# Groups of x centred by GpSimd, their maximum and rounding on VectorE a slot later, in a gated cross-attention and feed-forward block

## The chip, the core and the metric

The kernel runs on one core of a Trainium2 chip. The metric is device microseconds from the start to the end of one execution. The five engines have their own queues of instructions and run in order, each on its own: PE (TensorE), DVE (VectorE), ACT (ScalarE), POOL (GpSimd) and SP (SyncE, which here only issues transfers). They wait for each other by semaphores alone.

## What is computed

The reference, cut to what matters:

```python
x = x + tanh(g_xattn[0]) * xattn(layernorm(x), ctx, ctx)   # 32 batches, 112 rows, 256 wide; 375 keys; 16 heads
x = x + tanh(g_ffn[0]) * ffn(layernorm(x))

def ffn(x):                               # bitlinear: x -> 1024 (gate and up) -> 256
    return bitlinear(silu(bitlinear(x, w_gate)) * bitlinear(x, w_up), w_down)
def bitlinear(x, w):
    return einsum(act_quant(x), weight_quant(w))
def act_quant(x):                         # per row, to 255 levels
    scale = 127 / max(|x|)
    return clip(round(x * scale), -128, 127) / scale
```

The rows of the second layer normalisation are 32 x 112 = 3584, that is 28 tiles of 128 rows. A row is centred (its mean is taken off), and the levels are the rounded quotients of the centred row and a 127th of its largest magnitude. The standard deviation only enters the scale, later.

## The kernel before, in words

**Time is a table of slots.** All engines run through the same function `timeline`: slot t = 8n + p, where row n is a batch and p one of its eight slots (two heads each), from t = -16 to 302 and on; each engine issues in slot t what the code of that slot gives it, in the order in which it is written. The attention has two passes. The first (scores, their maximum, exponentials and statistics; L1328, L926, L1197, L907) ends with slot 257. The second (transposed scores L1369, exponentials L1187 into `pt`, weighted values L1348) runs 26 slots behind it, up to slot 282. Behind both come the batch's last steps, each in a fixed slot p: `ot` is copied (p = 2, L916), the output projection (p = 3, PE L1415), the new rows x2 are written (p = 4, DVE L885), the heads are turned back (p = 5, PE L1433), normalised (p = 6, DVE L891 and L895, the tile `on`), and POOL makes `onn`, `on` and `ong` (p = 7, L684, L685, L689: "the trio"). The value projections stand in p = 6, 7 and 0 on PE (L1407) and are copied a slot later by DVE (L859, the tile `va`); all of these use one PSUM bank `p_m`, in turn.

**The groups.** While the second pass runs out (slots 258 to 285, from 641 us on), the 28 row tiles of x2 are read back in groups of two tiles and made into levels. Groups 0 to 11 (`EARLY_GROUPS` + 1 = `TAILED` = 12 of them) are spread over the slots, group i from slot X_AT + 2i = 258 + 2i, by `group_at(t, lag)`; what follows for a group is at a fixed lag:

- lag -3: SP loads it into `xl` (part of the tile `ctxt`), two buffers (`load_group`, L457)
- lag 0: DVE takes the mean off (L990, into `fxn`, part of the tile `ex`), takes the largest magnitude of each row (L996, `xmax`), makes the scale (L998, `xsc`) and its inverse (L1000, `xinv`) (`x_group`)
- lag 1: ACT multiplies by the inverse and adds a large number, which rounds (L1233, `round_group`, in place)
- lag 2: POOL takes that number off again and writes bf16 (L728, `quant_group`, into `fxq`, part of `qp`)
- lag 3: PE transposes four blocks (L1485, `transpose_group`)
- lag 4: DVE copies them out of PSUM (L1015, `copy_group`, into parts of `kp`, `kf` and `ctxt`)

**The feed-forward** runs by tiles: `tile(0)` to `tile(7)` stand between slots 284 and 308 (`BETWEEN`), the others follow. In `tile(s)`: PE multiplies tile s by the gate and up weights (L1492), ACT makes silu (L1250, `sg`), DVE the product (L1032, part of the tile `kst`) and its row maximum (L1035), after every second tile also the scale and inverse (L1040, L1042); ACT rounds tile s - 2 (L1257), POOL takes the number off (L744), SP transposes by a DMA, and six tiles later PE multiplies by the third weights (L1524), ACT scales (L1243), POOL adds the residual (L751). For the last seven tiles DVE does that (L1053).

**The two late groups**, 12 and 13 (tiles 24 to 27), stand in the feed-forward: `LATE_AT = {10: 12, 13: 13}` puts the same steps of `x_group` at tile 10 and 13 of DVE, the rounding one tile later, and so on. For these DVE takes the mean off by another instruction, a scalar-tensor-tensor that adds a column of zeros in PSUM (L992), with a memset of that column before the first.

## Time and profile before

| | |
|---|---|
| median of three runs | 793.21 us (792.26 to 796.49) |
| the profiled execution | 792.8 us, its span 791.0 us |
| mean granted clock of TensorE, share of full speed | 0.962 |
| DVE busy | 708.0 us (90% of the span) |
| PE busy | 702.7 us (89%) |
| ACT busy | 683.9 us (86%) |
| POOL busy | 487.9 us (62%) |

The profile is of one execution. "Busy" is the time in which an instruction of the engine runs; the busy shares are means over stages with different limits. In the stage of the groups (640 to 688 us) all engines have gaps; in the feed-forward (688 to 781 us) DVE has nearly none. The page's map of the span in 40 slices of 19.8 us shows this (each digit the busy tenths): the last nine digits of DVE are 776798995, those of POOL 043245663.

### The profile page before, as it was taken

How to read it: one execution, taken by the hardware profiler on the slowest of the kernel's cores; microseconds unless marked ns; L12 is line 12 of the kernel's file. 1: busy time of each engine (PE TensorE's matmuls, PEld its weight loads, DVE VectorE, ACT ScalarE, POOL GpSimd, SP SyncE). 2: the span in 40 equal slices, each digit the busy share in tenths (PEclk: the TensorE clock that was granted, in tenths of full speed). 3: DMA queues.
4: the chain of work that ended last, by engine and by line, in shares of the span. 5: the costliest groups of instructions: out<-in, count | busy, mean ns of one | idle time of the engine just before them, and what ended most of it. 6: DMA issues, size and time to landing. Idle time of an engine off the chain costs nothing.

```text
span 791.0 us, 20866 instructions
## 1 busy us (share of the span) xinstructions
PE 702.7 (89%) x7118; PEld 474.6 (60%) x7127; DVE 708.0 (90%) x1452; ACT 683.9 (86%) x1454; POOL 487.9 (62%) x956
## 2 busy tenths in 40 slices
PE   6567899999999999999999999999999888877896
PEld 4334566666666666667676766676765555533453
DVE  5779899989899999999999999899999776798995
ACT  1578899898999999999999999999999888768883
POOL 4747657667777667676766666767664043245663
PEclk9666899999999999999999999999999899999998
DMA  9997747464668575767455666656664122246688
GB/s 206 204 261 166 197 127 149 109 126 128 154 120 149 124 144 124 145 122 158 123 138 134 134 137 133 128 136 130 124 118 85 39 68 86 71 103 164 160 179 181
DMA packets 148887, 108.50 MB, mean 137 GB/s; under 512 B 56991, under 2 KB 145183, under 8 KB 148767
## 3 DMA queue, kind: packets, MB, share of 16 engines
q1 hardware_dynamic: 143630, 101.98, 58.3%
q10 hardware_dynamic: 5152, 5.19, 2.7%
q8 instruction: 57, 0.93, 0.6%
q14 instruction: 48, 0.39, 0.2%
HBM read 49.54 MB, written 12.85 MB: 79 GB/s over the span
## 4 chain that ended last, share of the span: by engine, by line
PE 36%; ACT 35%; DVE 16%; issue 9%; DMA 2%; ACTq 1%; POOL 1%; SPq 0%; DVEq 0%; POOLq 0%
ACT ex L1197 13%; ACT pt L1187 12%; PE p_o L1348 7%; PE p_m L1426 6%; PE p_s L1328 5%; PE p_m L1407 5%; PE p_t L1369 4%; DVE kst L1032 3%; DVE hmax L1035 3%; PE p_m L1415 3%; ACT L1223 3%; ACT L1187 2%; DVE stats L907 2%; PE p_m L1399 2%; DVE nm L926 2%
## 5 line engine op out<-in xcount | busy, mean ns | idle before, releaser
L1197 ACT ACTIVATE ex<-p_s,nm 112x375 f32<-112x375 f32 x512 | 275.8, 618 | 12.3 <-DVE nm L926 11.0
L1187 ACT ACTIVATE pt<-p_t,ct 128x336 f32<-128x336 f32 x488 | 245.8, 577 | 26.7 <-PE p_t L1369 24.5
L907 DVE BATCH_NORM_STATS2 stats<-ex 112x6 f32<-112x375 f32 x512 | 252.5, 535 | 1.4 <-ACT ex L1197 1.3
L926 DVE TENSOR_REDUCE nm<-p_s 112x2 f32<-112x750 f32 x256 | 236.0, 922 | 1.2 <-PE p_s L1328 1.0
L1328 PE MATMUL p_s<-kst,qst 96*112 96x375 bf16 x512 | 154.8, 348 | 13.5 <-ACT ex L1197 7.3
L1369 PE MATMUL p_t<-qst,kst 99*128 99x112 bf16 x1464 | 115.1, 213 | 4.9 <-ACT pt L1187 4.0
L1369 PEld LDWEIGHTS p_t<-qst,kst 99*128 99x128 bf16 x1464 | 91.1, 98 | 44.0 <-issue 19.7
L1407 PE MATMUL p_m<-wv_sb,ctxt 128*128 128x256 f32 (+1 forms) x384 | 106.7, 401 | 4.7 <-DVE va L859 2.9
L1348 PE MATMUL p_o<-pt,va 128*32 128x112 f32 (+1 forms) x3072 | 101.7, 265 | 1.4 <-ACT pt L1187 0.8
L1426 PE MATMUL p_m<-ctxt,wk_sb 128*128 128x375 f32 x240 | 94.6, 518 | 1.7 <-DVE qf L875 1.1
L1328 PEld LDWEIGHTS p_s<-kst,qst 96*112 96x112 bf16 x512 | 67.0, 139 | 45.7 <-ACT ex L1197 34.6
L1348 PEld LDWEIGHTS p_o<-pt,va 128*32 128x32 f32 (+1 forms) x3072 | 70.4, 110 | 29.3 <-issue 27.0
L1407 PEld LDWEIGHTS p_m<-wv_sb,ctxt 128*128 128x128 f32 (+1 forms) x384 | 66.7, 190 | 20.4 <-DVE va L859 10.3
L859 DVE TENSOR_TENSOR va<-p_m,bv_sb 128x256 f32<-128x256 f32 (+1 forms) x96 | 40.0, 417 | 27.4 <-PE p_m L1407 26.6
L1426 PEld LDWEIGHTS p_m<-ctxt,wk_sb 128*128 128x128 f32 x240 | 44.3, 199 | 28.2 <-DVE x L885 7.5
L572 POOL TENSOR_SCALAR kp<-kf 128x375 bf16<-128x375 f32 x63 | 32.8, 521 | 43.9 <-ACT kf L1130 43.9
L578 POOL TENSOR_TENSOR kp<-kf,kp 128x375 bf16<-128x375 f32 x63 | 55.3, 878 | 5.2
L574 POOL TENSOR_TENSOR kf<-kf,kp 128x375 f32<-128x375 f32 x63 | 55.1, 875 | 5.3
L1492 PE MATMUL p_s<-wq,kp 128*128 128x512 bf16 x161 | 41.1, 380 | 12.6 <-DVE kst L1032 10.0
L744 POOL TENSOR_SCALAR kst<-kst 128x1024 bf16<-128x1024 f32 (+1 forms) x28 | 28.9, 1032 | 28.4 <-ACT kst L1257 28.3
L1257 ACT ACTIVATE kst<-kst,hinv 128x1024 f32<-128x1024 f32 (+1 forms) x29 | 32.1, 1115 | 9.0 <-DVE hinv L1042 9.0
L1032 DVE SCALAR_TENSOR_TENSOR kst<-p_s,usc,kst 128x1024 f32<-128x1024 f32 x28 | 35.9, 1282 | 3.6 <-ACT kst L1250 3.3
(187 smaller groups left out, 1164.3 us busy)
## 6 DMA issues: line engine op xcount, KB each, us to landing
kst<-kp SPq DMA_DIRECT2D x378, 93.8 KB, 3.5
ctxt<-ctxt_dram SPq DMA_DIRECT2D x32, 375.0 KB, 4.2
qbounce<-qp SPq DMA_DIRECT2D x32, 168.0 KB, 2.5
qst<-qbounce SPq DMA_DIRECT2D x32, 168.0 KB, 3.6
qst<-qbounce SPq DMA_DIRECT2D x32, 112.0 KB, 3.4
xm<-x_dram SPq DMA_DIRECT2D x32, 112.0 KB, 2.4
x_dram<-x SPq DMA_DIRECT2D x32, 112.0 KB, 1.9
xt<-x_dram SPq DMA_DIRECT2D x28, 128.0 KB, 3.2
```

The source lines that it names most:

```text
L574: nc.gpsimd.tensor_tensor(kf[:, c], kf[:, c], hi, ALU.subtract).then_inc(s_kx, 1)
L578: nc.gpsimd.tensor_tensor(lo, kf[:, c], mid, ALU.subtract).then_inc(s_kp2, 1)
L907: last = nc.vector.bn_stats(stats[:, nb % RING, 2 * pb + i], ex[0:SQ, 2 * (t % 2) + i, :])
L926: nc.vector.tensor_reduce(nm[:, n % RING, 2 * p:2 * p + 2], p_s[t % 2][0:SQ, :, 0:SK], axis=AX.X, op=ALU.max, negate=True).then_inc(s_max, 1)
L1032: nc.vector.scalar_tensor_tensor(out=hh[n % HHRING].rearrange("p (b k) -> p b k", b=2), in0=p_u[:, :, :], scalar=usc[:, n:n + 1], in1=sg[n ...
L1187: nc.scalar.activation(pt[:, (2 * r + i) % 8], st_home(r, i)[:, 0:KC * SQ].rearrange("k (c q) -> k c q", c=KC), ACT.Exp, scale=ct[:, nr % ...
L1197: nc.scalar.activation(ex[0:SQ, 2 * ((t - 1) % 2) + i, :], p_s[(t - 1) % 2][0:SQ, i, 0:SK], ACT.Exp, bias=nm[:, ne % RING, h:h + 1]).then_ ...
L1328: scores = mm(p_s[t % 2][0:SQ, i, 0:SK], qst[n % KRING][0:STACK, h, :], kst[n % KRING][0:STACK, h, 0:SK], start=True, stop=True)
L1348: last = mm(o_acc[VW * i:VW * (i + 1), grp, :], va[ng % VRING][0:KEYS[c], c, 4 * grp + i, :], pt[0:KEYS[c], (2 * (g - 1) + i) % 8, c, :], ...
L1369: last = mm(st_home(r, i)[:, c * SQ:(c + 1) * SQ], kst[nr % KRING][:, h, c * KR:(c + 1) * KR], qst[nr % KRING][:, h, :], start=True, stop= ...
L1407: last = mm(p_m[0:KEYS[ch], 0:D], ctxt[:, v % CRING, k, ch * KR:ch * KR + KEYS[ch]], wv[:, k, :], start=(k == 0), stop=(k == C - 1))
L1426: last = mm(p_m[:, 0:SK], wk[:, k, c * P:(c + 1) * P], ctxt[:, f % CRING, k, :], start=(k == 0), stop=(k == C - 1))
```

## The change

- POOL gets a new `centre_group` at lag 0: the two negated means of the group (128x2, L728 of the changed kernel; they are written into the columns of `xinv` that the inverses take later), then two tensor-scalars of 128x256, "add the negated mean, times 1.0", from `xl` to `fxn` (L737 there). It stands behind `quant_group` of the group before in the same slot.
- DVE's `x_group` moves from lag 0 to lag 1 and no longer takes the mean off. For groups 0 to 11 it then rounds the group itself, with two tensor-scalars of 128x256 in place, in the same slot. ACT's `round_group` is gone for them.
- The late groups: POOL centres them at tile 10 and 13, DVE takes maximum, scale and inverse at 11 and 14, ACT rounds at 12 and 15, POOL quantises at 13 and 16, PE transposes at 15 and 18, DVE copies at 16 and 19. The column of zeros and its memset are gone.
- SP's wait before loading group i is for the centring of group i - 2, as it was, but now POOL's.

```diff
@@ POOL, slot(t)
                 i = group_at(t, 2)
                 if i is not None:
                     quant_group(i)
+                i = group_at(t, 0)
+                if i is not None:
+                    centre_group(i)
+
+            def centre_group(i):
+
+                of = slice(GROUP * i, GROUP * (i + 1))
+                pool.wait_ge(s_ag, GROUP * (i + 1))
+                nc.gpsimd.tensor_scalar(xneg[:, of], mv2[:, of, 0], -1.0, 0.0, ALU.mult, ALU.add).then_inc(s_neg, 1)
+                pool.wait_ge(s_gl[i % 2], ring_count(16 * GROUP, i, 2))
+                if i == 0:
+                    pool.wait_ge(s_bn, SLOTS * B)
+                if i >= 2:
+                    pool.wait_ge(s_gq, count(1, i - 2, 1))
+                pool.wait_ge(s_neg, count(1, i, 1))
+                for g in range(GROUP):
+                    k = GROUP * i + g
+                    last = nc.gpsimd.tensor_scalar(fxn[:, i % 2, g], xl[:, i % 2, g], xneg[:, k:k + 1], 1.0, ALU.add, ALU.mult)
+                last.then_inc(s_cen, 1)
@@ POOL, tile(s)
-                if s - 2 in LATE_AT:
-                    quant_group(LATE_AT[s - 2])
+                if s - 3 in LATE_AT:
+                    quant_group(LATE_AT[s - 3])
+                if s in LATE_AT:
+                    centre_group(LATE_AT[s])
@@ DVE, slot(t)
-                i = group_at(t, 0)
+                i = group_at(t, 1)
                 if i is not None:
                     x_group(i)
@@ DVE, x_group(i)
-                for g in range(GROUP):
-                    k = GROUP * i + g
-                    if i < TAILED:
-                        last = nc.vector.tensor_scalar(fxn[:, i % 2, g], xl[:, i % 2, g], mv2[:, k, 0:1], None, ALU.subtract)
-                    else:
-                        last = nc.vector.scalar_tensor_tensor(out=fxn[:, i % 2, g], in0=xl[:, i % 2, g], scalar=mv2[:, k, 0:1],
-                                                              in1=zero.to_broadcast([P, D]), op0=ALU.subtract, op1=ALU.add)
-                last.then_inc(s_gx, 1)
-                dve.wait_ge(s_gx, count(4, i, 1))
+                dve.wait_ge(s_cen, count(1, i, 1))
                 nc.vector.tensor_reduce(xmax[:, of], fxn[:, i % 2], axis=AX.X, op=ALU.max, apply_absolute_value=True).then_inc(s_gx, 1)
...
+                if i < TAILED:
+                    dve.wait_ge(s_gx, count(3, i, 3))
+                    for g in range(GROUP):
+                        k = GROUP * i + g
+                        last = nc.vector.tensor_scalar(fxn[:, i % 2, g], fxn[:, i % 2, g], xinv[:, k:k + 1], ROUND, ALU.mult, ALU.add)
+                    last.then_inc(s_gr, 1)
@@ DVE, tile(s)
-                if s in LATE_AT:
-                    x_group(LATE_AT[s])
+                if s - 1 in LATE_AT:
+                    x_group(LATE_AT[s - 1])
@@ ACT, slot(t)
-                i = group_at(t, 1)
-                if i is not None:
-                    round_group(i)
@@ SP, load_group(i)
-                    sp.wait_ge(s_gx, count(4, i - 2, 1))
+                    sp.wait_ge(s_cen, count(1, i - 2, 1))
```

How the instructions stand now, at the places of which the prediction speaks. DVE, slots 260 to 262, before (from the new rows of slot 260 to the normalised heads of slot 262; group 0 stands ahead of them):

```order
L885 SCALAR_TENSOR_TENSOR x<-p_m,tg_sb,xm 112x256
L901 RECIPROCAL fa<-fa 112x32
L990 TENSOR_SCALAR ex<-ctxt,mv 128x256 x2
L996 TENSOR_REDUCE xmax<-ex 128x2
L998 TENSOR_SCALAR xsc<-xmax 128x2
L1000 RECIPROCAL xinv<-xsc 128x2
L931 BN_STATS st<-xt 128x6
L936 BN_AGGR mv<-st 128x2
L891 RECIPROCAL rl<-p_m 112x16
L895 TENSOR_TENSOR on<-p_m,rl 112x256
```

The same stretch of the changed kernel:

```order
L906 SCALAR_TENSOR_TENSOR x<-p_m,tg_sb,xm 112x256
L922 RECIPROCAL fa<-fa 112x32
L952 BN_STATS st<-xt 128x6
L957 BN_AGGR mv<-st 128x2
L999 TENSOR_REDUCE xmax<-ex 128x2
L1001 TENSOR_SCALAR xsc<-xmax 128x2
L1003 RECIPROCAL xinv<-xsc 128x2
L1008 TENSOR_SCALAR ex<-ex,xinv 128x256 x2
L912 RECIPROCAL rl<-p_m 112x16
L916 TENSOR_TENSOR on<-p_m,rl 112x256
```

Group 1 has moved from slot 260 to slot 261, behind the statistics (`st`, `mv`) and still ahead of `rl` and `on` of slot 262; its first instruction now reads what POOL has centred, and it ends with the rounding.

POOL before, from the last feature (`fc`, slot 258) to the trio of slot 263 (`fd` is of slot 260, the first `qp` is group 0):

```order
L663 TENSOR_TENSOR fc<-fc,fe 112x32
L667 TENSOR_TENSOR fd<-fa 112x32
L670 TENSOR_TENSOR fd<-fd,fc 112x32
L728 TENSOR_SCALAR qp<-ex 128x512 x2
L684 TENSOR_SCALAR onn<-on 112x256
L685 TENSOR_SCALAR on<-on 112x256
L689 TENSOR_TENSOR ong<-onn,on 112x256
L728 TENSOR_SCALAR qp<-ex 128x512
```

POOL from the same place on, in the changed kernel:

```order
L663 TENSOR_TENSOR fc<-fc,fe 112x32
L728 TENSOR_SCALAR xinv<-mv 128x2
L737 TENSOR_SCALAR ex<-ctxt,xinv 128x256 x2
L667 TENSOR_TENSOR fd<-fa 112x32
L670 TENSOR_TENSOR fd<-fd,fc 112x32
L747 TENSOR_SCALAR qp<-ex 128x512
L728 TENSOR_SCALAR xinv<-mv 128x2
L737 TENSOR_SCALAR ex<-ctxt,xinv 128x256 x2
L747 TENSOR_SCALAR qp<-ex 128x512
L728 TENSOR_SCALAR xinv<-mv 128x2
L737 TENSOR_SCALAR ex<-ctxt,xinv 128x256 x2
```

The centring of group 0 stands between `fc` and `fd`, and each further centring behind the quantising (L747) of the group before it: the two alternate, through all twelve groups.

## Rows read from the trace of the kernel before

**Rows 1.** Busy time in four stretches of the groups' stage (busy us, count, by engine)

```profile
core 0: us, PE busy (x) PEld busy (x) DVE busy (x) ACT busy (x) POOL busy (x), PEclk, DMA share, GB/s
...
sum 48.00, PE 38.38 PEld 28.05 DVE 34.98 ACT 40.97 POOL 17.99; mean PE 9.60 PEld 7.01 DVE 8.74 ACT 10.24 POOL 4.50
```

**Rows 2.** Busy time in the feed-forward stage, same columns

```profile
688.00:781.00 93.00, 75.84 (x433) 40.83 (x440) 86.36 (x124) 72.98 (x86) 50.69 (x70) 1.00 0.66 152
```

**Rows 3.** Groups by form, ACT, 640 to 688 us (busy us, mean ns; idle before)

```profile
L1233 ACT ACTIVATE ex<-ex,xinv 128x256 f32<-128x256 f32 x24 | 10.9, 506 | 3.7 <-DVE xinv L1000 3.6
```

**Rows 4.** The chain that ended last, 640 to 690 us, by line

```profile
by line: ACT pt L1187 13.4%; issue 10.2%; PE p_o L1348 9.3%; DVE xmax L996 7.0%; DVE ex L990 6.4%; PE p_m L1415 6.3%; ACT ex L1233 4.8%; PE p_m L1407 4.1%; PE p_s L1369 3.7%; DVE kp L1015 3.2%; PE p_t L1369 3.1%; PE p_s L1485 2.8%; DVE kst 
```

**Rows 5.** Groups by form, DVE, 640 to 688 us

```profile
L996 DVE TENSOR_REDUCE xmax<-ex 128x2 f32<-128x512 f32 x12 | 8.2, 686 | 0.4
...
L990 DVE TENSOR_SCALAR ex<-ctxt,mv 128x256 f32<-128x256 f32 x24 | 7.7, 361 | 0.0
...
L998 DVE TENSOR_SCALAR xsc<-xmax 128x2 f32<-128x2 f32 x12 | 2.8, 237 | 0.4
...
L1000 DVE RECIPROCAL xinv<-xsc 128x2 f32<-128x2 f32 x12 | 2.0, 166 | 0.4
```

**Rows 6.** Groups by form, POOL, whole span

```profile
L678 POOL TENSOR_SCALAR xn<-xa,mv,rstd 112x256 f32<-112x256 f32 x28 | 34.3, 1226 | 0.0
...
L621 POOL TENSOR_SCALAR ltc<-lt 128x32 f32<-128x32 f32 x16 | 5.2, 324 | 14.7 <-ACT lt L1155 14.7
...
L654 POOL TENSOR_SCALAR fe<-fb 112x32 f32<-112x32 f32 x16 | 3.5, 218 | 1.4
...
L693 POOL TENSOR_SCALAR bo_sb<-bo_sb,tg_sb 128x256 f32<-128x256 f32 x1 | 0.5, 477 | 0.0
```

**Rows 7.** Timeline, all engines, 640 to 664 us (start us, us, engine, line)

```profile
641.36 0.61 DVE L990 TENSOR_SCALAR ex<-ctxt,mv 128x256 f32<-128x256 f32 x2
...
642.03 0.25 POOL L663 TENSOR_TENSOR fc<-fc,fe 112x32 f32<-112x32 f32 x1
...
644.15 0.48 DVE L885 SCALAR_TENSOR_TENSOR x<-p_m,tg_sb,xm 112x256 f32<-112x256 f32 x1 [1.05 <-PE p_m L1415]
...
644.55 0.34 DVE L901 RECIPROCAL fa<-fa 112x32 f32<-112x32 f32 x1
...
645.63 0.62 POOL L728 TENSOR_SCALAR qp<-ex 128x512 bf16<-128x512 f32 x1
...
647.33 0.42 DVE L895 TENSOR_TENSOR on<-p_m,rl 112x256 f32<-112x256 f32 x1
...
653.39 0.97 ACT L1187 ACTIVATE pt<-p_t,ct 128x336 f32<-128x336 f32 x2
...
657.86 0.39 DVE L916 COPY ot<-p_s 128x224 f32<-128x224 f32 x1 [1.73 <-PE p_s L1319]
```

**Rows 8.** Timeline, all engines, 664 to 692 us

```profile
664.85 1.13 PE L1407 MATMUL p_m<-wv_sb,ctxt 128*128 128x256 f32 x4 [0.34 <-DVE on L895]
...
682.57 0.73 POOL L631 TENSOR_TENSOR xm<-xm,bo_sb 112x256 f32<-112x256 f32 x1
...
682.62 0.70 DVE L998 TENSOR_SCALAR xsc<-xmax 128x2 f32<-128x2 f32 x1
...
684.67 0.39 DVE L916 COPY ot<-p_s 128x224 f32<-128x224 f32 x1 [0.77 <-PE p_s L1319]
...
687.31 1.45 PEld L1492 LDWEIGHTS p_s<-wq,kp 128*128 128x128 bf16 x8
```

**Rows 9.** Groups of lines, DVE, 640 to 688 us: copies of the values

```profile
L859 DVE TENSOR_TENSOR va<-p_m,bv_sb 128x256 f32<-128x256 f32 (+1 forms) x6 | 2.5, 418 | 3.6 <-PE p_m L1407 3.6
```

**Rows 10.** Groups of lines, DVE, 688 to 781 us

```profile
L992 DVE SCALAR_TENSOR_TENSOR ex<-ctxt,mv,p_t 128x256 f32<-128x256 f32 x4 | 1.7, 477 | 0.0
...
L998 DVE TENSOR_SCALAR xsc<-xmax 128x2 f32<-128x2 f32 x2 | 1.1, 532 | 0.1
```

**Rows 11.** Transfers, 640 to 690 us (KB, us from issue to landing)

```profile
ctxt<-x_dram SPq DMA_DIRECT2D x20, 128.0 KB, 2.2
```

More of the change, by code:

```diff
@@ L144, in gated_block @@
         xmax, xsc, xinv = sb("xmax", [P, TILES]), sb("xsc", [P, TILES]), sb("xinv", [P, TILES])
+        xneg = xinv
         gsc, usc = sb("gsc", [P, TILES]), sb("usc", [P, TILES])
@@ L214, in gated_block @@
         tail_ride = p_s[0][:, 1, 0:C * SQ].rearrange("p (c q) -> p c q", c=C)
-        zero = p_t[0][:, 511:512]
         p_g, p_u = p_s[0], p_s[1]
@@ L263, in gated_block @@
         s_sc0, s_raw, s_raw2, s_smallw = sem("s_f_scaled_by_pool"), sem("s_f_unclipped"), sem("s_f_unclipped_by_pool"), sem("s_setup_weights")
-        s_zero = sem("s_zero_column")
+        s_neg, s_cen = sem("s_f_means_negated"), sem("s_f_x_centred")
         s_bn2, s_ln2, s_sq2 = sem("s_f_bn"), sem("s_f_ln"), sem("s_f_sqrt")
@@ L967, in rows_scale @@
                 dve.wait_ge(s_ln2, count(3, j, 2))
-                dve.wait_ge(s_gx, count(4, end // GROUP))
+                dve.wait_ge(s_gx, count(3, end // GROUP))
                 nc.vector.tensor_tensor(rstd2[:, first:end], rstd2[:, first:end], xsc[:, first:end], ALU.mult).then_inc(s_ln2, 1)
@@ L976, in x_group @@
                 of = slice(GROUP * i, GROUP * (i + 1))
[L977 to L995 removed]
+                dve.wait_ge(s_cen, count(1, i, 1))
                 nc.vector.tensor_reduce(xmax[:, of], fxn[:, i % 2], axis=AX.X, op=ALU.max, apply_absolute_value=True).then_inc(s_gx, 1)
[L997 removed]
+                dve.wait_ge(s_gx, count(3, i, 1))
                 nc.vector.tensor_scalar(xsc[:, of], xmax[:, of], XSC_MIN, 1.0 / 127.0, ALU.max, ALU.mult).then_inc(s_gx, 1)
[L999 removed]
+                dve.wait_ge(s_gx, count(3, i, 2))
                 nc.vector.reciprocal(xinv[:, of], xsc[:, of]).then_inc(s_gx, 1)
+                if i < TAILED:
[4 more added lines that the diff above has]
+                    last.then_inc(s_gr, 1)
             def copy_group(i):
@@ L1022, in tile @@
                     rows_scale(EARLY_TILES, TILES, 1)
-                if s - 5 in LATE_AT:
-                    copy_group(LATE_AT[s - 5])
+                if s - 6 in LATE_AT:
+                    copy_group(LATE_AT[s - 6])
                 n = s
@@ L1223, in slot @@
                     nc.scalar.activation(hid1[:, :], t_h1, ACT.Gelu, bias=b1[:, 0:1]).then_inc(s_g1, 1)
-                i = group_at(t, 1)
-                if i is not None:
-                    round_group(i)
             def round_group(i):
-                act.wait_ge(s_gx, count(4, i, 4))
+                act.wait_ge(s_gx, count(3, i, 3))
                 for g in range(GROUP):
@@ L1257, in tile @@
                         nc.scalar.activation(hr[n % HRING][:, half], hh[n % HHRING][:, half], ACT.Copy, scale=hinv[:, n:n + 1], bias=ROUND).then_inc(s_hr, 1)
-                if s - 1 in LATE_AT:
-                    round_group(LATE_AT[s - 1])
+                if s - 2 in LATE_AT:
+                    round_group(LATE_AT[s - 2])
                 if s == SQ_AT:
@@ L1530, in tile @@
                         nc.tensor.matmul(p_u[:, 0, :], identb[:, :], wq8[0][:, 0:512], start=True, stop=True)
-                if s - 4 in LATE_AT:
-                    if LATE_AT[s - 4] == TAILED:
+                if s - 5 in LATE_AT:
+                    if LATE_AT[s - 5] == TAILED:
                         pe.wait_ge(s_otc, B)
-                    transpose_group(LATE_AT[s - 4])
+                    transpose_group(LATE_AT[s - 5])
             timeline(slot, tile)
```

12 lines of the change are left out of this document (removed).

## The prediction

> **What bounds the kernel now.** The page first: DVE, PE and ACT are each busy for 86 to 90% of the span, so the whole tells nothing, and the stages have to be read apart. Then the stretches. In the 48 us of the groups' stage ACT is busy for 41 us, PE for 38, DVE for 35 and POOL for 18 [rows 1]: ACT is the fullest, none is full. In the feed-forward DVE is busy for 86.4 of 93 us [rows 2]: DVE sets the pace there, and POOL, busy for 51, has room.
>
> For the groups' stage the question is what ended last. Of the chain over 50 us the exponentials L1187 have 13.4%, PE's weighted values 9.3%, DVE's maximum 7.0% and centring 6.4%, ACT's rounding 4.8% [rows 4]. So the chain runs across the engines, and rounding on ACT was on it for 4.8% of 50 us, 2.4 us, though it fills ACT for 10.9 us [rows 3]. That gives what relieving ACT can bring by itself: near 2.4 us, and 10.9 only if ACT were the bound all through.
>
> **What is removed.** From ACT 24 roundings, 10.9 us [rows 3]. From DVE 24 centrings, 7.7 us [rows 5], and four late ones of 477 ns, 1.9 us [rows 10], with a small memset.
>
> **What is added, and what a group costs now.** On DVE 24 roundings take the place of the 24 centrings: the same form, 128x256 to 128x256 with a pointer, so 0.36 us each by L990 [rows 5], with those in it that POOL held up; two back to back, undisturbed, take 0.61 us [rows 7]. DVE's work for an early group is as large as before: maximum 0.69, scale 0.17, inverse 0.17, two roundings 0.62, and with the handovers between them 1.73 us.
>
> On POOL a group gets the negation and two centrings. The negation of two columns I take at 0.2 us by the small multiply-add L654 (0.218) [rows 6]. The centring is an operation that the trace of before does not show: add by pointer, times an immediate. Its bounds are the two rows of the same 256 elements: multiply by pointer and add, 0.477 us (L693), and subtract and multiply by two pointers, 1.226 us (L678) [rows 6]. Below 0.4 there is no row of this size. L621 (maximum, then minimum, 32 elements) takes 0.324 us where L654 takes 0.218 for as many: 0.106 over 32 elements is 3.3 ns more for each, and L678 against L693 is (1.226 - 0.477) / 256 = 2.9 ns more for each. So there are two speeds by pair of operations, and no row says to which add-multiply belongs. I take the fast one, 0.45 us each, because it is nearest in form to L693 (one pointer, one immediate, a sum and a product), and keep 1.23 for a rival. The Trainium skill (GPSIMD Engine Reference, section 7) says that bodies of up to two operations on an element should run at the port's rate, about one cycle an element; L678 disagrees with it, two operations at 4 ns an element, so here the rows decide. By that page the sum stays at the fast price.
>
> **A new loop.** This is the main term. POOL centres group i behind the quantising of group i - 1, in its queue; that waits for DVE's rounding of i - 1; DVE's group i waits for the centring. Before, DVE never waited for POOL's last group, only for the one before it. Now twelve groups run strictly in turn: quantise 0.62 [rows 7], negate 0.2, centre twice 0.85 to 0.9, DVE 1.73, handovers of some 0.2: **3.6 us a group**. The slots of before ran from the `ot` copy at 657.86 to the one sixteen slots (eight groups) on at 684.67 [rows 7, 8], 26.8 us or 3.35 us a group. So the loop is slower than the stage was, and it holds DVE's queue: `ot`, the new rows, `on` and the value copies stand behind a group that waits for POOL.
>
> - *Head.* POOL is busy with the features until 642.28 (L663) [rows 7]. Centring 0 ends at 643.4, DVE's group 0 at 645.1, L885 and L901 (0.48 and 0.34, overlapping a little) at 645.9 instead of 644.9 [rows 7], POOL's two `fd` and the quantising at 647.2, centring 1 at 648.4, DVE's group 1 at 650.1, and `on` starts at 650.4, not at 647.33 [rows 7]. PE's value projection waits for it, the second hidden layer stands behind that projection, and two table loads of ACT behind the hidden layer. The layer could not have come at once before either, since it waited for ACT, so of 3.1 us I carry 2.3: the exponentials start again at 655.7, not at 653.39 [rows 7]. **+2.3 us.**
> - *Rounds.* Four groups are a round of eight slots, 4 x 3.6 = 14.4 us. Two more things delay it. The group of slot 7 now stands behind the first value copy: `on`, the projection of 1.13 us [rows 8] and a copy of 0.42 [rows 9] take 2.3 us where POOL takes 1.8, +0.45. And the trio runs on POOL beside that group: `xsc` took 0.70 us where its usual is 0.17, when POOL had a tensor-tensor of 0.73 under way (L631) [rows 8], and `ong` is one of the same size; I take +0.35, and +0.1 for the last value copy. 15.3 against 13.4 us, twice, less 0.5 for the last round, which has no projections: **+3.3 us.**
> - *End.* Before, the first feed-forward matmul began 2.6 us after the last `ot` copy of the stage (684.67 to 687.31) [rows 8], as PE waited for ACT's exponentials. ACT is now ahead, and only the projection of 1.1 us lies between: **-1.1 us.**
>
> For the clash of DVE and POOL the Trainium skill has a harder rule (SBUF — State Buffer, section "Who interferes with whom"): one engine locks the shared ports for a whole instruction, and the other waits it out. The row agrees, 0.70 us beside an instruction of 0.73. By the rule alone the trio could cost its whole rest behind the maximum, 0.8 us a round, which would add 1 us to the sum.
>
> SP's wait before a load is for the centring two groups ahead, some 6 us before the data is wanted; a load lands 2.2 us after issue [rows 11]. Nothing.
>
> **Feed-forward.** DVE loses 4 x 0.477 = 1.9 us [rows 10], and DVE is the bound, so all of it counts. POOL's work for a late group, 1.1 us twice, goes into its gaps; what it delays is the quantising of a tile, whose result is wanted several tiles later. The later places of the groups' steps cost nothing: the copies end at tiles 16 and 19, and tile 24 is the first to read them. The scale L998 took 0.53 us there on average [rows 10], held up by POOL; that can go either way by 0.5 each. **-1.9 us.**
>
> Sum: 2.3 + 3.3 - 1.1 - 1.9 = +2.6 us on the profiled execution's 792.8: 795.4. The median of the runs is 793.2, 0.4 above the profiled one; I say **795.5 us**. With each term off by up to its half, this case alone spans 791 to 800.
>
> **The rivals.**
>
> - *Add-multiply is a slow pair on POOL (L678's speed).* Then each centring costs 0.75 us more, and with the loop binding 24 x 0.75 = 18 us, of which some 2 are already counted as waits for values and the trio: 812. Against it: L693. For it: subtract-multiply is the nearest pair of arithmetic, and that is slow. In the feed-forward POOL's two groups would take 1.5 us more each, in its gaps.
> - *ACT's relief pays and the loop does not bind.* If quantising and centring overlap more than the rows allow, or the slots absorb the wait, the stage gains the 2.4 us of rounding on the chain [rows 4], and the feed-forward its 1.9: 788.5, faster. Against it: the loop's 3.6 us is made of durations in the rows and of a queue order that leaves no overlap. For it: ACT is the fullest engine of the stage [rows 1], and PE takes a group's blocks only at lag 3, a slack of one slot.
> - *The late groups give nothing.* If ACT or PE takes over as the bound at tiles 10 to 15, the 1.9 us stay, and the time is 797.3. This lies within my case's own range.
>
> That the change does not do what it says can be left out: the instructions stand as the order shows.
>
> **How the numbers follow.** Half a per cent (4 us) is about what a measurement of this kernel tells from no change, so faster means under 789.2 and slower over 797.2. My case has 0.63: slower 0.19, same 0.43, faster 0.01. The slow pair has 0.25, all slower. The relief has 0.12: faster 0.08, same 0.04. Together faster 0.09, same 0.47, slower 0.44. The range must reach to the slow pair, as 0.25 is too much to leave out: 791 to 813. It leaves out the relief and what lies above 813.
>
> **What would show it.** The duration of L737: near 0.45 or near 1.23 us. Group to group on POOL: 3.6 us or more between the quantisings, each group of DVE starting as the centring ends, with POOL's wait for DVE's rounding next to it. `on` of slot 262 some 3 us later than 647.3; first feed-forward matmul near 692. ACT with long gaps in the stage. From there to the end some 2 us less than before. I am wrong if DVE's maxima start without waiting for POOL, if the stage ends before 688, or if the feed-forward keeps its length.

## The result and the profile after

| | before | after |
|---|---|---|
| median of seven runs each, on one chip | 793.14 us (789.69 to 796.49) | 799.02 us (796.55 to 800.12) |
| ratio | | 1.0067, 95% interval 1.0035 to 1.0099 |
| the profiled execution, and its span | 792.8, 791.0 us | 796.55, 794.5 us |
| mean granted clock of TensorE | 0.962 | 0.951 |
| ACT busy | 683.9 us | 673.8 us |
| POOL busy | 487.9 us | 500.4 us |

Slower, by 5.3 us if the ratio is put on 793.2 (the medians differ by 5.9). The measured median is 3.5 us above the forecast of 795.5 and inside its range of 791 to 813.

The groups by form, 640 to 700 us, answer to [rows 3, 5, 6] (busy us, mean ns; then the idle time before them and what ended it):

```profile
L737 POOL TENSOR_SCALAR ex<-ctxt,xinv 128x256 f32<-128x256 f32 x24 | 11.2, 477 | 2.3 <-POOL xinv L728 2.3
...
L999 DVE TENSOR_REDUCE xmax<-ex 128x2 f32<-128x512 f32 x12 | 8.2, 682 | 10.9 <-POOL ex L737 10.9
L1008 DVE TENSOR_SCALAR ex<-ex,xinv 128x256 f32<-128x256 f32 x24 | 7.8, 365 | 0.4
L1413 PE MATMUL p_m<-wv_sb,ctxt 128*128 128x256 f32 x16 | 7.7, 634 | 5.7 <-DVE on L916 5.7
L747 POOL TENSOR_SCALAR qp<-ex 128x512 bf16<-128x512 f32 x12 | 7.4, 618 | 17.5 <-DVE ex L1008 17.5
```

The disputed price is the fast one, 477 ns. The loop is there from both of its sides: POOL's quantising waited 17.5 us for DVE's rounding, DVE's maximum 10.9 us for POOL's centring; in the kernel before the maximum waited for nothing of POOL's [rows 5]. The fourth line is one that no step of the prediction had: the value projections waited 5.7 us for `on`.

One turn of the loop undisturbed, in the timelines of the two engines (start us, us). POOL:

```profile
664.17 0.62 POOL L747 TENSOR_SCALAR qp<-ex 128x512 bf16<-128x512 f32 x1 [1.86 <-DVE ex L1008]
664.76 0.19 POOL L728 TENSOR_SCALAR xinv<-mv 128x2 f32<-128x2 f32 x1
665.15 0.94 POOL L737 TENSOR_SCALAR ex<-ctxt,xinv 128x256 f32<-128x256 f32 x2 [0.20 <-POOL xinv L728]
667.94 0.62 POOL L747 TENSOR_SCALAR qp<-ex 128x512 bf16<-128x512 f32 x1 [1.86 <-DVE ex L1008]
```

DVE in the same stretch:

```profile
666.12 0.69 DVE L999 TENSOR_REDUCE xmax<-ex 128x2 f32<-128x512 f32 x1 [0.69 <-POOL ex L737]
666.84 0.17 DVE L1001 TENSOR_SCALAR xsc<-xmax 128x2 f32<-128x2 f32 x1
667.04 0.17 DVE L1003 RECIPROCAL xinv<-xsc 128x2 f32<-128x2 f32 x1
667.24 0.62 DVE L1008 TENSOR_SCALAR ex<-ex,xinv 128x256 f32<-128x256 f32 x2
```

From one quantising to the next it takes 3.77 us; the maximum starts as the centring ends (665.15 + 0.94 = 666.09), the quantising as the rounding ends. Neither engine is full, and no two of the loop's steps overlap.

**Landmarks of the stage.** The `ot` copies of slots 258, 266, 274 and 282 and the first product of the feed-forward cut the stage into three intervals of eight slots and an end. Before, by DVE's timeline (two of these lines are among [rows 7, 8]):

```profile
641.05 0.39 DVE L916 COPY ot<-p_s 128x224 f32<-128x224 f32 x1 [1.05 <-PE p_s L1319]
...
672.62 0.39 DVE L916 COPY ot<-p_s 128x224 f32<-128x224 f32 x1 [1.01 <-PE p_s L1319]
...
689.57 1.28 DVE L1032 SCALAR_TENSOR_TENSOR kst<-p_s,usc,kst 128x1024 f32<-128x1024 f32 x1 [1.36 <-ACT kst L1250]
```

After:

```profile
639.92 0.39 DVE L937 COPY ot<-p_s 128x224 f32<-128x224 f32 x1 [1.04 <-PE p_s L1325]
...
660.23 0.38 DVE L937 COPY ot<-p_s 128x224 f32<-128x224 f32 x1
...
676.98 0.38 DVE L937 COPY ot<-p_s 128x224 f32<-128x224 f32 x1
...
692.44 0.38 DVE L937 COPY ot<-p_s 128x224 f32<-128x224 f32 x1
...
698.01 1.28 DVE L1041 SCALAR_TENSOR_TENSOR kst<-p_s,usc,kst 128x1024 f32<-128x1024 f32 x1 [2.07 <-ACT kst L1256]
```

| interval, us | 258 to 266 | 266 to 274 | 274 to 282 | 282 to first product | sum |
|---|---|---|---|---|---|
| before | 16.81 | 14.76 | 12.05 | 4.90 | 48.5 |
| after | 20.31 | 16.75 | 15.46 | 5.57 | 58.1 |

So the stage is 9.6 us longer, each part of it. From the first product to the last (28 tiles) it is 86.24 us before (689.57 to 775.81) and 83.04 after (698.01 to 781.05), 3.2 less; what lies behind the last product is 1.7 less (15.2 and 13.5), and the stage began 1.1 earlier. That is 9.6 - 3.2 - 1.7 - 1.1 = 3.6, the span's 3.5. The last two are not the change's: over all the traces below the first `ot` copy lies between 639.2 and 643.9 us though nothing ahead of it differs, and behind the last product the granted clock was 0.74 and 0.50 before (windows from 784 to 792 us), 0.64 and 0.93 after. So I compare inside the stage, and leave the whole to the timed ratios.

**The clock.** The windows by 4 us show what the mean of 0.951 hides (busy us and count by engine, then the granted clock as a share of 2.4 GHz):

```profile
644.00:648.00 4.00, 2.30 (x42) 1.62 (x32) 1.93 (x6) 2.69 (x5) 2.18 (x6) 1.00 0.29 92
648.00:652.00 4.00, 2.22 (x8) 1.67 (x9) 2.10 (x11) 0.00 (x0) 2.48 (x6) 0.58 0.33 102
652.00:656.00 4.00, 4.00 (x37) 2.76 (x34) 2.35 (x7) 3.14 (x5) 2.40 (x5) 0.57 0.22 66
656.00:660.00 4.00, 3.83 (x61) 3.00 (x61) 2.15 (x8) 3.90 (x11) 1.05 (x3) 1.00 0.23 66
...
668.00:672.00 4.00, 3.44 (x13) 2.61 (x14) 2.53 (x9) 0.97 (x2) 3.15 (x7) 0.64 0.36 114
...
684.00:688.00 4.00, 2.22 (x36) 2.08 (x40) 2.85 (x10) 1.80 (x5) 2.87 (x7) 0.77 0.39 121
688.00:692.00 4.00, 2.72 (x42) 1.65 (x34) 2.27 (x8) 0.43 (x2) 2.75 (x6) 0.50 0.00 0
692.00:696.00 4.00, 3.03 (x10) 1.95 (x11) 2.89 (x12) 1.66 (x2) 0.62 (x1) 0.50 0.01 4
```

PE waited just before each fall (PE's timeline; the last line lies inside the third stretch, where the clock is already low):

```profile
649.78 2.07 PE L1413 MATMUL p_m<-wv_sb,ctxt 128*128 128x256 f32 x4 [2.89 <-DVE on L916]
...
668.53 1.57 PE L1413 MATMUL p_m<-wv_sb,ctxt 128*128 128x256 f32 x4 [2.83 <-DVE on L916]
...
685.78 0.38 PE L1491 MATMUL p_s<-identb_sb,qp 128*128 128x128 bf16 x4 [2.31 <-DVE kf L1024]
...
692.97 2.02 PE L1421 MATMUL p_m<-wo_sb,ot 128*112 128x256 f32 x4 [1.19 <-DVE ot L937]
```

A projection takes 2.07 us where it took 1.13 [rows 8]. The clock had gone to its lower level, 1.2 GHz; the first two falls follow waits that the new loop makes. In the trace of before it was 1.00 all through the stage, and the prediction did not ask what a longer wait on PE would do to it. The Trainium skill (TensorE: Matmul & The Clock Gate, Part 1) says that the clock has these two levels and falls when the array has been idle; the trace agrees.

### The profile page after: what moved, and what is told of

Read it like the earlier page. It is cut to its first block, busy times and chain, and to the rows that moved or that the text cites. A ratio compares the mean times of both kernels' runs of the same rounds, so it can differ in the third digit from the quotient of the medians.

```text
span 794.5 us, 20887 instructions
## 1 busy us (share of the span) xinstructions
PE 708.9 (89%) x7127; PEld 480.6 (60%) x7127; DVE 704.7 (89%) x1447; ACT 673.8 (85%) x1430; POOL 500.4 (63%) x998
## 4 chain that ended last, share of the span: by engine, by line
PE 46%; ACT 21%; DVE 19%; issue 8%; POOL 2%; DMA 2%; ACTq 1%; SPq 0%; DVEq 0%; POOLq 0%
PE p_m L1432 9%; PE p_o L1354 8%; ACT ex L1206 8%; PE p_s L1334 6%; ACT pt L1196 5%; PE p_t L1375 5%; PE p_m L1413 5%; DVE kst L1041 4%; PE p_m L1421 3%; DVE stats L928 3%; DVE hmax L1044 3%; ACT L1232 2%; ACT L1196 2%; DVE nm L947 2%; PE p_m L1405 2%
## 5 line engine op out<-in xcount | busy, mean ns | idle before, releaser
L1413 PE MATMUL p_m<-wv_sb,ctxt 128*128 128x256 f32 (+1 forms) x384 | 109.6, 409 | 8.2 <-DVE on L916 6.5
L1432 PE MATMUL p_m<-ctxt,wk_sb 128*128 128x375 f32 x240 | 92.6, 508 | 1.8 <-DVE qf L896 0.9
L1334 PEld LDWEIGHTS p_s<-kst,qst 96*112 96x112 bf16 x512 | 66.7, 139 | 45.4 <-ACT ex L1206 35.2
L1405 PE MATMUL p_m<-xnt,wq_sb 128*128 128x112 f32 x256 | 39.1, 301 | 0.6 <-DVE xnt L944 0.6
```

Source lines behind the costliest of these rows:

```text
L1334: scores = mm(p_s[t % 2][0:SQ, i, 0:SK], qst[n % KRING][0:STACK, h, :], kst[n % KRING][0:STACK, h, 0:SK], start=True, stop=True)
L1413: last = mm(p_m[0:KEYS[ch], 0:D], ctxt[:, v % CRING, k, ch * KR:ch * KR + KEYS[ch]], wv[:, k, :], start=(k == 0), stop=(k == C - 1))
L1432: last = mm(p_m[:, 0:SK], wk[:, k, c * P:(c + 1) * P], ctxt[:, f % CRING, k, :], start=(k == 0), stop=(k == C - 1))
```

## The experiments

All are ratios to the kernel before, timed in turn with it on the same chip; the chip differs from one batch of experiments to the next. The intervals of the stage stand in one table at the end.

**e1_late_only**: the early groups as before, the two late ones as changed. In `slot(t)` and `x_group` the lines of the kernel before come back for i < TAILED:

```diff
-                i = group_at(t, 1)
+                i = group_at(t, 0)
                 if i is not None:
                     x_group(i)
@@ POOL, slot(t)
-                i = group_at(t, 0)
-                if i is not None:
-                    centre_group(i)
```

> Only the two late groups are changed; groups 0 to 11 are as before. Both theories: the groups' stage keeps the length of before (first feed-forward product L1032 to first ot copy as before), the feed-forward is 3 us shorter than before, as in the changed kernel (83.0 us from its first to its last product against 86.2). Ratio to before 0.996 (790 us), faster by 0.3 to 0.5%.

Measured: 792.06 us, **0.9958** (0.993 to 0.9986). **e2_early_only** is the opposite: the early groups as changed, the late ones with L992, its zeros and DVE's old places (`if s in LATE_AT: x_group(LATE_AT[s])`).

> Only groups 0 to 11 are changed; the late groups are as before. Whatever the mechanism, this holds the whole loss: 3 us more than the changed kernel, ratio to before 1.010 to 1.012 (801 to 803 us); feed-forward 86.2 us from first to last product.

Measured: 803.45 us, **1.0103** (1.0063 to 1.0144). The product of the two is 1.0061, the changed kernel 1.0067: the two parts add up. The late part gains 0.4%, the early part loses 1.0%. One expectation missed: e2's feed-forward took 87.7 us, not the 86.2 of before. Its steps from product to product are those of before to 0.01 us but for one, 4.02 us for 2.57, and there the clock had fallen. PE's wait ahead of it and a window, e2:

```profile
738.40 1.04 PE L1518 MATMUL p_s<-wq,kp 128*128 128x512 bf16 x4 [2.00 <-DVE kst L1061]
...
740.00:744.00 4.00, 4.00 (x19) 2.03 (x18) 2.51 (x3) 2.73 (x4) 2.50 (x4) 0.66 0.53 137
```

The same place in the kernel before:

```profile
728.19 1.04 PE L1492 MATMUL p_s<-wq,kp 128*128 128x512 bf16 x4 [2.00 <-DVE kst L1032]
...
728.00:732.00 4.00, 3.63 (x20) 1.89 (x21) 3.85 (x6) 3.32 (x5) 1.22 (x2) 1.00 0.57 144
```

The same wait of 2.00 us was followed by a fall in one execution and by none in the other.

**e3_swap**: POOL centres group i before it quantises group i - 1.

```diff
@@ POOL, slot(t)
-                i = group_at(t, 2)
-                if i is not None:
-                    quant_group(i)
                 i = group_at(t, 0)
                 if i is not None:
                     centre_group(i)
+                i = group_at(t, 2)
+                if i is not None:
+                    quant_group(i)
```

> The changed kernel, but POOL centres group i before it quantises group i - 1, so that a centring no longer waits for DVE's rounding of the group before. Loop theory: DVE's waits for POOL (10.9 us over 8) fall under 3 us, `on` is no longer late, PE's waits of 2.9 us for it go and with them the half clock, and the stage is back to the length of before or 1 to 2 us shorter; ratio to before 0.993 to 0.997. Rival (the cost is the group's place a slot later on DVE, or DVE's and POOL's clashes on SBUF, which grow here as both now run at once): still 1.004 or more.

Measured: 791.86 us, **0.9951** (0.9923 to 0.9979). The same instructions, in another order on one engine, are 1.2% faster than the change. In its timeline POOL runs ahead:

```profile
662.18 0.94 POOL L737 TENSOR_SCALAR ex<-ctxt,xinv 128x256 f32<-128x256 f32 x2 [0.20 <-POOL xinv L728]
...
663.38 0.62 DVE L1008 TENSOR_SCALAR ex<-ex,xinv 128x256 f32<-128x256 f32 x2
...
664.09 0.62 POOL L747 TENSOR_SCALAR qp<-ex 128x512 bf16<-128x512 f32 x1 [0.96 <-DVE ex L1008]
664.61 0.68 DVE L999 TENSOR_REDUCE xmax<-ex 128x2 f32<-128x512 f32 x1
```

The quantising follows the rounding at 664.09, and the next group's maximum starts at 664.61 with no wait, since its centring (662.18) is long done. The second and third intervals fall by 3.5 and 4.1 us, the first stays (20.06). Not all came as expected: DVE's maxima still wait 4.2 us for POOL, in three waits, the clock still falls in the head (0.55 and 0.59 from 652 to 660 us), and the stage is 2.4 us longer than before, while the ratio is the one expected.

**e4_dve_rounds**: the kernel before, but DVE rounds its groups and ACT does not. There is no loop through POOL's centring, and POOL's own work is unchanged.

```diff
@@ DVE, x_group(i)
+                if i < TAILED:
+                    dve.wait_ge(s_gx, count(4, i, 4))
+                    for g in range(GROUP):
+                        k = GROUP * i + g
+                        last = nc.vector.tensor_scalar(fxn[:, i % 2, g], fxn[:, i % 2, g], xinv[:, k:k + 1], ROUND, ALU.mult, ALU.add)
+                    last.then_inc(s_gr, 1)
@@ ACT, slot(t)
-                i = group_at(t, 1)
-                if i is not None:
-                    round_group(i)
```

> The kernel before, with ACT's rounding of groups 0 to 11 moved to DVE behind the inverse in the same slot; DVE centres too, and POOL only quantises, so there is no loop through POOL, and ACT is relieved by 10.9 us. Loop theory: relief of ACT brings at most the 2.4 us that the rounding had on the chain, and DVE's extra 7.4 us (12 x 0.62) sits ahead of `on` and the value copies: 0 to +4 us, ratio 1.000 to 1.005. Rival (the loss comes from emptying ACT and from rounding on DVE, not from POOL): as bad as e2, 1.008 or more.

Measured: 800.17 us, **1.0062** (1.0033 to 1.0091), over what I expected and nearly as slow as the change. ACT's 10.9 us of rounding [rows 3] went, and the stage grew by 6.5 us: DVE's group now takes 2.35 us with the rounding in it. What stands behind it in DVE's queue, value copies and copies of levels, is what PE waits for in its trace (3.6 us for the value copies, 6.9 for the copies of levels), and its clock too falls to 0.50 in two places. The feed-forward is 2.5 us longer as well (88.8 us), around windows with the clock at 0.64. So relieving ACT doesn't pay where DVE takes the work; what the relief is worth by itself, and how the 6.5 us divide between DVE's queue and the clock, is not shown.

**e5_fill**: the changed kernel with idle matmuls on PE, whose results nothing reads: 16 before the first value projection of slots 262 and 270, 12 before the transposes of slots 279 and 281.

```diff
+            def keep_busy(where, t):
+
+                for _ in range(FILL.get((where, t), 0)):
+                    nc.tensor.matmul(p_s[0][:, 1, 256:512], identb[:, :], wq8[0][:, 0:256], start=True, stop=True)
```

> The changed kernel with idle matmuls (128x256, bf16, 107 ns each at full clock) on PE just ahead of four of its waits: 16 before the first value projection of slots 262 and 270, 12 before the transposes of slots 279 and 281. They go into gaps of 1 to 2.9 us and compute nothing. Theory A (the loop alone costs; PE's clock is a by-product): the stage keeps its 58.1 us from the ot copy of slot 258 to the first product, or loses 1 us at most; ratio to before 1.005 to 1.008. Theory B (a large part of the loss is that PE's waits let the granted clock fall to half for about 20 us of the stage, and the projections and weighted values then take twice as long on the path): the clock stays at 1.00, the stage takes 52 to 54 us, ratio to before 0.999 to 1.003.

Measured: 796.27 us, **1.0021** (0.9992 to 1.0051). In its trace the clock stays at 1.00 until 688 us, and the projection behind the wait takes 1.13 us again:

```profile
648.15 1.91 PE L1284 MATMUL p_s<-wq,identb_sb 128*128 128x256 bf16 x16
651.20 1.13 PE L1424 MATMUL p_m<-wv_sb,ctxt 128*128 128x256 f32 x4 [1.14 <-DVE on L918]
```

The first and second intervals are 1.34 and 1.29 us shorter than the changed kernel's, the third is the same, and the clock falls behind it all the same (0.87, 0.50, 0.78 from 688 to 700). So some 2.6 us of the 9.6 are the clock's in the trace, of which this kernel gives 0.9 back at the end. The stage of 56.4 us lies between what the two theories expected (57 to 58, and 52 to 54): the clock is a part of the loss, by this trace the smaller one. The two ratios' intervals overlap, so the timed runs alone would not prove it; and the profiled execution was the slowest of its twelve (800.75 us), with a feed-forward 1.4 us longer than after.

**e6_slow_pair**: the same value by subtracting the mean instead of adding its negative.

```diff
-                    last = nc.gpsimd.tensor_scalar(fxn[:, i % 2, g], xl[:, i % 2, g], xneg[:, k:k + 1], 1.0, ALU.add, ALU.mult)
+                    last = nc.gpsimd.tensor_scalar(fxn[:, i % 2, g], xl[:, i % 2, g], mv2[:, k, 0:1], 1.0, ALU.subtract, ALU.mult)
```

> The changed kernel, but POOL centres by subtracting the mean, times 1.0 (the negation is still made and not read). Loop theory, if the pair subtract-multiply runs at L678's speed: 1.23 us a centring for 0.477, 1.5 us a group more, the loop goes from 3.77 to 5.3 us, and of 12 x 1.5 = 18 us some 3 are absorbed by waits that are there anyway: 13 to 17 us over the changed kernel, ratio to before 1.023 to 1.028. If POOL's centring were not on the path of each group: within 3 us of the changed kernel. If the pair is fast and only two pointers are slow: no change.

Measured: 812.92 us, **1.0230** (1.0179 to 1.0281), the stage 12.7 us longer than after. Groups by form, 640 to 715 us:

```profile
L737 POOL TENSOR_SCALAR ex<-ctxt,mv 128x256 f32<-128x256 f32 x24 | 27.3, 1145 | 2.3 <-POOL xinv L728 2.3
L999 DVE TENSOR_REDUCE xmax<-ex 128x2 f32<-128x512 f32 x12 | 8.2, 685 | 22.0 <-POOL ex L737 21.9
```

1145 ns against 477 for the same tile and operand kinds: the speed goes by the pair of operations. The second interval grows by 4.0 us for four groups, 1.0 each of the 1.3 that a group's centring grew, the third by 5.3, all of it. This was the rival of 812 us, and it is what the kernel would be, had the writer not negated the mean first.

**e7_hybrid**: e3, and groups 0 and 1 as in the kernel before (DVE centres them in their own slot, ACT rounds them; HEAD is 2).

```diff
@@ DVE, slot(t)
+                i = group_at(t, 0)
+                if i is not None and i < HEAD:
+                    x_group(i)
                 i = group_at(t, 1)
-                if i is not None:
+                if i is not None and i >= HEAD:
                     x_group(i)
@@ ACT, slot(t)
+                i = group_at(t, 1)
+                if i is not None and i < HEAD:
+                    round_group(i)
```

> e3 (POOL centres before it quantises), but groups 0 and 1 as in the kernel before (DVE centres in their own slot, ACT rounds). Loop theory: the head's loss goes (20.1 us in e3 from the ot copy of slot 258 to that of slot 266 against 16.8 before), the rounds of e3 stay (13.3 and 11.4 us against 14.8 and 12.1), so the stage is 2 us shorter than before and the ratio to before 0.988 to 0.993. If the head was late by something else (the tables, the clock): 0.995 as e3.

Measured: 787.21 us, **0.9907** (0.9871 to 0.9943). The first interval is back at 16.67, and the stage at 47.5 us, 1.0 under the kernel before (I expected 2; its end, with the clock down, is 6.08 us against 4.90). **e9_hybrid_loop** puts the changed kernel's order on POOL back into it (quantise, then centre), to see whether head and loop are two losses.

> As e7_hybrid (groups 0 and 1 as in the kernel before), but with the changed kernel's order on POOL in the steady loop: quantise group i-1, then centre group i. Theory (head and loop are two separate losses): the interval between the ot copies of slots 258 and 266 comes back to about 16.8 us (20.31 in the changed kernel, 16.67 in e7), the two later ones stay at 15.5 to 16.8 (13.36 and 11.37 in e7). That is 3.3 to 3.5 us better than the changed kernel: ratio to the kernel before about 1.002 (1.000 to 1.004). Rival A (one effect: the order on POOL alone made both): near the changed kernel's 1.0067. Rival B (the head alone cost it, the loop hides elsewhere): near e7's 0.991.

Measured: 795.42 us, **1.0007** (0.9983 to 1.0032). 16.63, 16.72 and 15.50 us: the head of e7, the loop of the change, as the theory had it.

**e8_late_fill**: e1 with 8 and 4 idle matmuls ahead of the transposes of slots 279 and 281, since e1's own trace has the half clock at its end. Its early groups are those of the kernel before, and so is PE's wait near the end of the stage (e1, then before):

```profile
683.07 0.38 PE L1500 MATMUL p_s<-identb_sb,qp 128*128 128x128 bf16 x4 [0.99 <-DVE kf L1030]
```

```profile
681.49 0.38 PE L1485 MATMUL p_s<-identb_sb,qp 128*128 128x128 bf16 x4 [0.99 <-DVE kf L1015]
```

Behind it the clock fell in e1 (0.71, 0.50, 0.93 from 684 to 696 us; end 7.09 us) and held in the profiled execution of before (end 4.90).

> e1 (only the late groups changed) with 8 idle matmuls before the transposes of slot 279 and 4 before those of slot 281, where e1's profile has PE waiting 1.0 and 0.2 us and then the clock at half from 686 to 693 us. Theory B: the clock holds through the end of the stage, which becomes 2 us shorter than e1's: ratio to before 0.992 to 0.994. Theory A, or gaps too small to matter: 0.996 to 0.998.

Measured: 790.7 us, **0.9948** (0.9925 to 0.9971), against e1's 0.9958. The end shrank from 7.09 to 4.72 us in the trace; in the timed runs no difference shows. **e10_hybrid_fill** does the same to e7 (4, 8 and 4 in slots 277, 279 and 281).

> e7_hybrid with idle matmuls (their results are used by nothing) ahead of the transposes of slots 277 (4), 279 (8) and 281 (4), where TensorE waited 1.11 and 1.63 us in e7 before its granted clock fell (0.78, 0.50, 0.87 of full from 680 to 692 us). Theory (the waits make the clock fall, and the half clock costs 1 to 2 us at the end of the stage): granted clock 1.00 through the end of the stage, last interval 4.7 to 5.0 us instead of 6.08, ratio to the kernel before 0.988 to 0.990. Rival (the clock there costs nothing, DVE or ACT ends last anyway): 0.991 as e7, or up to 0.992 by the added matmuls.

Measured: 787.34 us, **0.9904** (0.9873 to 0.9935), the end 4.13 us instead of 6.08. Both were then run side by side.

> The same kernel as e7_hybrid, run on one chip with its variant with idle matmuls (e12), since the two were timed on different days of the study and their ratios to the kernel before (0.9907 and 0.9904) differ by less than either interval, while their traces differ by 1.95 us at the end of the stage (6.08 against 4.13 us from the last ot copy to the first product). Theory (the end of the stage passes on to the end of the kernel): this run's median lies 1.5 to 2.5 us above e12's. Rival (what is gained there is lost behind it, or the timed executions without a profile do not have the half clock): the two medians within 0.5 us.

> The same kernel as e10_hybrid_fill, beside e11 on one chip. Theory: 1.5 to 2.5 us below e11's median, ratio to the kernel before 0.986 to 0.990. Rival: within 0.5 us of e11, both near 0.990.

Measured: 786.76 us (0.9903, 0.9868 to 0.9939) and 787.20 us (0.9903, 0.987 to 0.9936). The rival is right: no gain in the timed runs, though the two traces differ as the first pair did. Windows of e11, without the added matmuls:

```profile
676.00:680.00 4.00, 2.37 (x46) 1.78 (x42) 3.16 (x10) 1.83 (x4) 3.31 (x7) 0.78 0.02 5
680.00:684.00 4.00, 4.00 (x35) 2.75 (x34) 2.68 (x11) 1.81 (x2) 0.62 (x1) 0.50 0.00 0
```

The same stretch of e12:

```profile
676.00:680.00 4.00, 3.06 (x58) 2.33 (x59) 3.23 (x9) 2.00 (x5) 3.57 (x8) 1.00 0.04 9
680.00:684.00 4.00, 3.36 (x40) 2.08 (x41) 3.15 (x14) 2.03 (x3) 0.64 (x2) 1.00 0.05 15
```

The end is 1.9 us shorter (6.00 to 4.12), the feed-forward the same (83.05 and 83.04 from first to last product), what lies behind the last product 1.0 us longer (14.3 and 15.3), and the spans differ by 0.6. In that last stretch e12 has the lower clock (0.74 and 0.50 from 776 us to its end, against 0.73 and 0.85 from 772 to 780 and then 1.00 in e11): there it gives back some of what the added matmuls had kept. Where the rest of it stays in the executions without a trace is open.

| interval, us | 258-266 | 266-274 | 274-282 | end | stage | feed-forward | ratio |
|---|---|---|---|---|---|---|---|
| before | 16.81 | 14.76 | 12.05 | 4.90 | 48.5 | 86.2 | 1 |
| after | 20.31 | 16.75 | 15.46 | 5.57 | 58.1 | 83.0 | 1.0067 |
| e1 late only | 16.82 | 14.75 | 12.42 | 7.09 | 51.1 | 83.1 | 0.9958 |
| e2 early only | 20.33 | 17.54 | 15.49 | 5.74 | 59.1 | 87.7 | 1.0103 |
| e3 swap | 20.06 | 13.29 | 11.39 | 6.12 | 50.9 | 83.1 | 0.9951 |
| e4 DVE rounds | 19.17 | 15.61 | 14.67 | 5.61 | 55.1 | 88.8 | 1.0062 |
| e5 fill | 18.97 | 15.46 | 15.46 | 6.49 | 56.4 | 84.4 | 1.0021 |
| e6 slow pair | 22.99 | 20.79 | 20.80 | 6.21 | 70.8 | 84.0 | 1.0230 |
| e7 hybrid | 16.67 | 13.36 | 11.37 | 6.08 | 47.5 | 83.1 | 0.9907 |
| e8 late fill | 16.79 | 14.75 | 12.24 | 4.72 | 48.5 | 83.1 | 0.9948 |
| e9 hybrid loop | 16.63 | 16.72 | 15.50 | 5.69 | 54.5 | 83.1 | 1.0007 |
| e10 hybrid fill | 16.68 | 13.29 | 11.38 | 4.13 | 45.5 | 83.1 | 0.9904 |
| e11 hybrid again | 16.66 | 13.28 | 11.36 | 6.00 | 47.3 | 83.1 | 0.9903 |
| e12 hybrid fill again | 16.66 | 13.28 | 11.36 | 4.12 | 45.4 | 83.0 | 0.9903 |

The feed-forward is taken from the first product to the last.

## Why the prediction was right, and where it was wrong

The mechanism was the predicted one, and the time fell in the range; that the point came within 3.5 us is in part luck. On the traces the terms were off by +5.1 us in the stage, by -1.3 in the feed-forward and by -2.8 at the two ends of the kernel, which the change doesn't touch, and these nearly cancel: 796.55 us against the 795.4 that the sum gave for the profiled execution. The range reached to 813 for a rival that did not come, and by the prediction's own bound for "slower", 797.2, it held "same" (0.47) a little likelier than "slower" (0.44), more than half of that for the slow pair. Two small slips in its sums: 795.4 and the 0.4 between the executions make 795.8, and the relief's 788.5 is 788.9 on the same footing. Of its signs, `on` came 3.1 us late as said (with the stage's earlier start of 1.1 taken in); the first weights of the feed-forward were loaded at 695.1 us, not near 692, and from there to the end it was 4.3 us less, not some 2.

- **The loop** was the mechanism, and e3 shows it. A turn is 3.77 us, not 3.6: the pair of centrings is 0.94, not 0.85 to 0.9, and between the negation and it lies a handover of 0.20 that I had folded into "some 0.2" for all. The round was said to be 15.3 us; it was 16.75 and 15.46. Two rounds cost +5.4, not +3.3. With the clock held (e5) both rounds are 15.46 and cost +4.1, so 1.3 of the missing 2.1 is the half clock at 668 to 672 us. The other 0.8 is less than eight turns at 0.17 more (1.4): what stood beside the loop, the copies and the trio, was taken some 0.6 too large.
- **The head.** `on` was due at 650.4; it started at 649.30 in a stage that began 1.13 us earlier, so at 650.43 on the clock of before. From there the step failed: the exponentials started 3.7 us late, not 2.3. The value projections ran at the lower clock level (2.07 us twice), and ACT stood for 6.08 us ahead of the second hidden layer. With the clock held (e5) the interval is 2.2 us over before: the 2.3 is right at full clock. e9 shows the head as a loss of its own, 3.7 us with the clock in it.
- **End, -1.1.** Wrong, and the worst step in kind: it measured +0.7. I gave the last projection its duration of before, 1.1 us [rows 8]; it took 2.02, behind a wait of 1.19 and with the clock at 0.50. With the clock held in e10 the end is 4.13, 0.8 under before. That speaks for the cover (ACT ahead) and for the clock as what took it back; but e10 is another kernel, and in the changed one no run held the clock there (e5's end is 6.49), so for this step it is argued, not shown. Nor is it a longer wait alone: e1's clock fell there behind the waits of before.
- What all three miss is **one term, the clock: the price of a wait on PE can be more than the wait.** The stage came out at +9.6 in place of 2.3 + 3.3 - 1.1 = +4.5. Of the missing 5.1 us e5 gives 2.6 to the clock in the head and the first round; 0.8 is the longer turn; 1.8 is the end, where the clock is likely; the head was 0.1 too large.
- **The feed-forward, -1.9**, measured -3.2. DVE's share of a late group fell from 2.24 us (724.61 to 726.85) and 2.60 us (735.36 to 737.96) to 1.08 and 1.37, together 2.4: the four L992 at 477 ns, the handovers behind them, the memset, and a scale held up for less time (0.30 and 0.76 us before, 0.17 and 0.45 after). DVE before and after at the second late group:

```profile
735.36 0.87 DVE L992 SCALAR_TENSOR_TENSOR ex<-ctxt,mv,p_t 128x256 f32<-128x256 f32 x2
736.26 0.69 DVE L996 TENSOR_REDUCE xmax<-ex 128x2 f32<-128x512 f32 x1
736.98 0.76 DVE L998 TENSOR_SCALAR xsc<-xmax 128x2 f32<-128x2 f32 x1
```

```profile
744.80 0.68 DVE L999 TENSOR_REDUCE xmax<-ex 128x2 f32<-128x512 f32 x1
745.51 0.45 DVE L1001 TENSOR_SCALAR xsc<-xmax 128x2 f32<-128x2 f32 x1
```

  The remaining 0.8 us lie between tiles 10 and 19; before and behind them every step from product to product is the same to 0.01 us. Half of it is in the tiles' own scales (13 of 225 ns before, L1040, of 196 ns after, L1049); the rest I cannot place. The rival "the late groups give nothing" is out: e1 is 0.42% faster by them alone.
- **DVE and POOL side by side.** The trio's cost was taken at 0.35 us a round: beside `ong` the scale took 0.34 us at 671.26 (0.17 alone), and the rounding pair 0.98 at 687.77 (0.62 alone). The extra is 0.17 and 0.36, so the size was right, small against the loop. The scale of 671.26 ended at 671.60 and `ong` at 671.57, as in [rows 8] the scale ended with L631 (683.32 and 683.30): that agrees with the rule, named in the prediction, by which one engine waits out the other's instruction. The whole rest of 0.8 did not come because the scale began when most of `ong` was over.
- **The rival of ACT's relief** had 0.12. As the kernel stands it is out: the loop binds (e3). e4 gives ACT the whole relief too, at the price of DVE's rounding, and is slower. But with the loop undone and the head as before (e7), the two middle intervals are 1.4 and 0.7 us under the kernel before, 2.1 in all, close to the 2.4 us that the chain gave the rounding [rows 4]. That fits a gain from the relief, under a loop that cost more. No run separates it from the centring on POOL and the groups' later place on DVE, which e7 has too.
- The sums: after against before, the order on POOL costs 7.5 us in the two later intervals (after less e3), the head 3.7 (after less e9), and e7, without both, is 10.6 us shorter in the stage than after. e7's ratio is worth 7.4 us, while its trace against that of before gives 1.0 in the stage and 3.2 in the feed-forward. The difference is in which executions were profiled: that of before (792.8 us) is 2.6 us under the median beside e7, that of e7 (789.15) 1.9 over its own.
- **By its mean clock the kernel before, too, is at the lower level for longer in most of its executions than in its trace.** Of the 80 that were timed beside e1 to e12, the 21 with a mean granted clock of 0.960 or more took 788.8 to 793.5 us, the 46 with 0.955 or less took 793.5 to 799.7. The profiled one had 0.962. All seven of the changed kernel lie at 0.944 to 0.952. So the one trace of before shows it at its better, and the stage's +9.6 us sets a trace with the clock down against one without. Where an ordinary execution of before loses it no trace shows; e1 lost it at the end of the stage and e2 at tile 12, both where their instructions are those of before.

## What to carry to other kernels

When a step moves to another engine, write down the order in that engine's queue and ask whether the step it stands behind is waiting for the very engine that it should feed: here two steps in the other order were worth 1.2%. Price a move on the queue of the receiving engine at its start too, where it may still be busy with other work (groups 0 and 1), and keep the old way for those. Where a change makes TensorE wait longer in a busy stretch, look at the granted clock behind the wait, and give the work there the duration that it has at the lower level as the other end of the range. Look at the mean clock of all timed executions before taking one trace as the kernel's own: here those at a low mean clock took 5.6 us more in the median than those at a high one.
